# Combine step of a fused attention and mixture layer: the elementwise product moved from GpSimd to VectorE

## The reference

```python
def _L0_attn_ref(content, Wq, Wk, Wv):          # 16 heads of 64
    Q = (content @ Wq).reshape(b, n, HEADS, HEAD_DIM)
    ...
    alpha = jax.nn.softmax(scores, axis=-1)
    alpha = jnp.where(causal, alpha, 0)          # masked after the softmax
    Y = jnp.einsum('bhqk,bkhd->bqhd', alpha, V).reshape(b, n, d)

def _L0_ffn_ref(...):                            # 8 gated experts round one causal attention, D = 128
    ...
    final = jnp.einsum('td,edc,te->tc', attn_out, o_proj, m * routing_weights)

xn = _layernorm(x, axis=-1)
s = _L0_attn_ref(xn, Wq, Wk, Wv)
g = _silu(_L0_ffn_ref(xn, sim_matrix, gates, q_proj, k_proj, v_proj, o_proj))
x = x + s * g
```

## Time and profile before

| | us |
|---|---|
| median of 2 runs | 3610.29 (3608.92 to 3611.66) |
| the profiled execution, its time | 3607.75 |
| its span on the slowest core (core 3), first to last instruction | 3606.2 |
| spans of the 8 cores | 3596.3 to 3606.2 |
| busy in the span: TensorE, VectorE, ScalarE, GpSimd | 2543.5, 2252.2, 2116.6, 324.7 |

### The profile page before, as it was taken

One profiled execution on the slowest core, in us unless ns is written; L12 is line 12 of the kernel. 1 busy time (PEld: TensorE's weight loads), 2 busy tenths in 40 slices (PEclk: granted clock), 3 DMA queues, 4 the chain that ended last, 5 costly groups with the idle time before them and its releaser, 6 DMA issues.

```text
span 3606.2 us, 59910 instructions; the slowest of 8 cores (3596.3 to 3606.2 us)
## 1 busy us (share of the span) xinstructions
PE 2543.5 (71%) x18642; PEld 1154.0 (32%) x18642; DVE 2252.2 (62%) x5858; ACT 2116.6 (59%) x2466; POOL 324.7 (9%) x738
## 2 busy tenths in 40 slices
PE   2179997673887777778778777777878777754430
PEld 1134444331333333333333333333333333321210
DVE  7457773232466766776676677677667667754542
ACT  0000005320277977986897797789679769965541
POOL 0100000000000100010010010001001000122233
PEclk9999998897888778778867867876886787655555
DMA  5510000114000000000000000000000000022334
GB/s 151 141 36 1 1 1 1 65 50 166 12 3 4 6 6 3 4 7 3 4 9 3 3 6 6 4 4 7 2 4 6 6 3 4 7 72 97 119 132 143
DMA packets 35777, 117.12 MB, mean 32 GB/s; under 512 B 5778, under 2 KB 5778, under 8 KB 35474
## 3 DMA queue, kind: packets, MB, share of 16 engines
q1 hardware_dynamic: 22738, 71.34, 5.6%
q0 software_dynamic: 12736, 41.95, 4.2%
HBM read 79.72 MB, written 33.55 MB: 31 GB/s over the span
## 4 chain that ended last, share of the span: by engine, by line
PE 31%; ACT 20%; DVE 17%; issue 15%; DMA 9%; DVEq 4%; POOLq 2%; POOL 1%; ACTq 0%; SPq 0%
ACT expC L1344 6%; ACT stagef L1359 6%; PE PB L889 5%; PE PB L903 5%; PE PB L874 5%; DVE cacc L1083 4%; PE PB L803 4%; DMA KTt<-s_sp 4%; PE PB L806 3%; PE PB L818 3%; PE PB L761 3%; ACT stagef L1344 3%; ACT R L1359 3%; DVE tmpc L1207 3%; POOLq L574 2%
## 5 line engine op out<-in xcount | busy, mean ns | idle before, releaser
L1207 DVE TENSOR_REDUCE tmpc<-stagef 128x2 f32<-128x1024 bf16 (+2 forms) x726 | 811.3, 1126 | 246.3 <-ACT stagef L1359 180.1
L1344 ACT ACTIVATE expC<-PB 128x1024 bf16<-128x1024 f32 x768 | 863.6, 1125 | 87.2 <-PE PB L889 87.2
L1359 ACT ACTIVATE stagef<-PB 128x1024 bf16<-128x1024 f32 x600 | 676.3, 1127 | 240.0 <-PE PB L903 138.4
L889 PE MATMUL PB<-R 64*128 64x512 bf16 x1152 | 296.4, 503 | 274.8 <-ACT stagef L1359 158.9
L1207 DVE TENSOR_REDUCE tmpc<-R 128x2 f32<-128x1024 bf16 (+2 forms) x362 | 406.1, 1122 | 117.6 <-ACT R L1359 89.5
L1344 ACT ACTIVATE stagef<-PB 128x1024 bf16<-128x1024 f32 x384 | 434.8, 1132 | 72.8 <-PE PB L889 72.8
L1359 ACT ACTIVATE R<-PB 128x1024 bf16<-128x1024 f32 x296 | 334.0, 1129 | 104.3 <-PE PB L903 58.4
L889 PE MATMUL PB<-QTt,KTt 64*128 64x512 bf16 x1152 | 283.7, 481 | 147.9 <-ACT stagef L1359 78.6
L683 PE MATMUL PB<-R,xnT 128*128 128x512 bf16 x1536 | 338.3, 380 | 1.0 <-DVE lnat L1000 0.9
L903 PE MATMUL PB<-R 64*128 64x512 bf16 (+3 forms) x1088 | 261.7, 473 | 50.2 <-ACT expC L1344 20.8
L1324 ACT ACTIVATE expC<-PB 128x512 bf16<-128x512 f32 x144 | 74.8, 612 | 364.0 <-PE PB L727 363.9
(11 more groups left out here) (162 smaller groups left out, 3012.0 us busy)
## 6 DMA issues: line engine op xcount, KB each, us to landing
stagef<-x SPq DMA_DIRECT2D x64, 512.0 KB, 4.2
out<-Vau SPq DMA_DIRECT2D x32, 512.0 KB, 4.5
g_sp<-stagef SPq DMA_DIRECT2D x32, 256.0 KB, 2.0
s_sp<-s_stage POOLq DMA_DIRECT2D x64, 128.0 KB, 2.4
QTt<-g_sp POOLq DMA_DIRECT2D x32, 256.0 KB, 3.0
KTt<-s_sp POOLq DMA_DIRECT2D x32, 256.0 KB, 4.1
R<-qp POOLq DMA_DIRECT2D x8, 512.0 KB, 5.2
R<-kp POOLq DMA_DIRECT2D x8, 512.0 KB, 4.8
```

Source lines behind the costliest of these rows:

```text
L889: last = e.matmul(POOL[it["slot"]][:, h * 512:h * 512 + 512], stat, mv, start=True, stop=True, tile_position=(64 * h, 0))
L1207: e.tensor_reduce(s.tmpc[:].rearrange("p (h c) -> p h c", h=2)[:, :, c:c + 1], s.c1scr((m1 - 1) % 3)[:, 0:2 * kw] .rearrange("p (h k) -> p ...
L1344: e.activation(s.expCs(es), PB[[0, 1, 3][it["slot"]]][:, :], AF.Exp).then_inc(sem["aC2"], 1)
L1359: e.activation(scr[:, 0:1024], pbsrc[:, 0:1024], AF.Exp).then_inc(sem["aC1"], 1)
```

## The change

GpSimd no longer waits for the two loads and no longer multiplies: for each tile it issues the two loads and goes on. VectorE waits for the two loads itself, multiplies `KT` by `QT` into `xnb`, drains, and adds as before. The condition under which GpSimd may issue the loads (`vCM` at least k2 - 1) is the same as before, and so are SyncE's list, the buffers and the two slots. The semaphore `gCM` is no longer used.

```diff
 def vector_cmb_one(self, e, j, b):
         e.wait_ge(sem["dCX0" if sl == 0 else "dCX1"], 16 * (k2 // 2 + 1))
-        e.wait_ge(sem["gCM"], k2 + 1)
+        e.wait_ge(sem["dCG0" if sl == 0 else "dCG1"], 16 * (k2 // 2 + 1))
+        e.wait_ge(sem["dCS0" if sl == 0 else "dCS1"], 16 * (k2 // 2 + 1))
         if k2 >= 2:
             e.wait_ge(sem["dOut0" if sl == 0 else "dOut1"], 16 * (k2 // 2))
+        e.tensor_tensor(s.xnb[:, sl * 1024:sl * 1024 + 1024],
+                        s.KT[:, sl * 1024:sl * 1024 + 1024],
+                        s.QT[:, sl * 1024:sl * 1024 + 1024],
+                        ALU.mult)
+        e.drain()
         e.tensor_tensor(vauo[:, sl * 1024:sl * 1024 + 1024],
                         s.xnb[:, sl * 1024:sl * 1024 + 1024],
                         xb[sl], ALU.add).then_inc(sem["vCM"], 1)
...
 def gpsimd_cmb_q(self, e, j):
             e.dma_start(s.KT[:, sl * 1024:sl * 1024 + 1024],
                         sr[:, i, :]).then_inc(sem["dCS0" if sl == 0
                                               else "dCS1"], 16)
-            e.wait_ge(sem["dCG0" if sl == 0 else "dCG1"], 16 * (k2 // 2 + 1))
-            e.wait_ge(sem["dCS0" if sl == 0 else "dCS1"], 16 * (k2 // 2 + 1))
-            e.tensor_tensor(s.xnb[:, sl * 1024:sl * 1024 + 1024],
-                            s.KT[:, sl * 1024:sl * 1024 + 1024],
-                            s.QT[:, sl * 1024:sl * 1024 + 1024],
-                            ALU.mult)
-            e.drain().then_inc(sem["gCM"], 1)
```

## The result

The changed kernel took 3518.17 us (median), the kernel before 3611.03 us beside it. The ratio is 0.9738, with a 95% interval of 0.9726 to 0.9750: 2.6% faster. The medians differ by 92.9 us, where the prediction said 114. The profiled execution has its slowest core at 3516.4 us (core 2) against 3606.2, so 89.8 us less.

The account below looks back on a forecast made before the run. A chain of latencies in the last head pair's combines was taken as the bound: 202.4 + 9.5 us of waits removed, less 73 remaining, less 24.6 of VectorE work, is 114; 3607.75 - 114 = 3494 us, range 3470 to 3530.

Parts of the forecast that it names:

- 202.4 + 9.5 of waits removed: Last head pair: VectorE's 202.4 us of waits for GpSimd's drain and 9.5 us for ScalarE would go.
- A: Combines of the last head pair: two tiles in flight, slightly slowed; 3480 to 3510 us, most likely 3494; chance 0.65.
- Rival B: Combines: DMA becomes bound, 3510 to 3537 us; sign: waits naming `out` or over 4 us at tiles 2, 3; chance 0.16.
- The path: Last head pair: VectorE's 202.4 us of waits set the time; windows between combines, with ScalarE full, keep their length.
- The product: VectorE, each of 32 tiles: product 0.69 us and drain 0.08, 24.6 us of added work in all.
- Block 1: Combine of block 1: VectorE's 9.5 us wait for ScalarE, behind GpSimd's late masks, would go.
- E: Each block's combine: the moment the normalization ends, from which times count; four tiles forecast to end 21.6 us later.
- The waits that remain: VectorE's waits for loads in the eight combines: 7 x 8.6 + 12.9 = 73 us.
- Tile 2 needs x, which is what lands last: Third tile of a block: x takes 5.3 us to land, plus 1.0 for sharing; a wait of 2.4 us.
- Rival C: Combines: transfers faster than in the kernel before, as the product no longer spaces them badly; 3471 to 3480 us; chance 0.10.
- Rival D: Combines: each tile still costs a full round trip, only the shorter product gains, 55 us, giving 3553 us; chance 0.06.
- Rival E: Combines: VectorE's operations hold up GpSimd's load issues, 4.0 us per tile, 128 in all, giving 3622 us; chance 0.03.

Follow-up runs that it names:

- e10_two_early: Changed kernel, two tiles in flight, but GpSimd issues loads once the product of two tiles earlier is through, not its addition; ratio 0.9758, 3508.71 us profiled.
- e3_no_x: Changed kernel with 30 of the 32 loads of x left out; ratio 0.9671, 3484.64 us profiled.
- e2_serial: Changed kernel with one tile in flight: GpSimd issues loads only after the previous tile's addition; ratio 0.9999, 3609.44 us profiled.
- e9_serial_early: Changed kernel with one tile in flight, loads issued once the previous tile's product is through, not its addition; 3551.97 us profiled.
- e1_ahead: Kernel before with the product left on GpSimd, but the next tile's loads issued ahead, two tiles in flight; ratio 0.9842, 3543.82 us profiled.
- e4_sp_queue: Changed kernel with the loads of g and s issued by SyncE instead of GpSimd; ratio 0.9720, 3509.25 us profiled.

## Why the prediction was right, and by how much it was not

The sum reads, with what was measured on the slowest cores: 202.4 + 9.5 of waits removed, less 98.1 that remain, less 24.6 of product and drain: 89.2 us, and the profiled spans differ by 89.8. So every term but one had its size. That one term moved the time out of the band of the forecast: 3518.17 us is outside A's 3480 to 3510, which had 0.65, and inside B's 3510 to 3537, which had 0.16. It lies within the whole range of 3470 to 3530 only because that range took in most of B.

- **The path.** Right. The waits of VectorE in the last head pair were on the path in full, and the stretches between the combines kept their length (148.0 and 146.7 us in all) with ScalarE full.
- **The product.** 690 ns and 0.08 for the drain (3239.88 + 0.69 to 3240.65), as taken. This agrees with the Trainium skill's rate for two bf16 inputs ("VectorE: DVE Perf Modes", the perf-mode tier table) and with its 150 fixed cycles.
- **Block 1.** Right. The first mask stands 15.0 us behind E (13.9 forecast), and the wait of 9.5 us for ScalarE is gone: no sum waits over 1.5 us for ScalarE there.
- **The waits that remain.** Wrong in size: 98.1 us in place of 73. On core 2, 56.8 us fall on the first tiles (47 forecast) and 41.3 on the others (26 forecast). On the other seven cores these are 48.9 to 57.0 and 37.3 to 42.2 us. So the second part was too small on every core, and the first by 2 to 4 us on four cores and by 10 on two, the slowest among them. The second part is the step "Tile 2 needs x, which is what lands last", with 1.0 and 1.5 us added for sharing: from the end of tile 0 to the start of tile 2's product the sum had 6.8 us, and the eight blocks took 7.2 to 9.0, 8.1 in the mean. I had read the landing of s, 3.0 to 4.4 us, off rows in which it was issued ahead of the store and of the load of x; in the changed kernel it is issued behind them, and lands in 5.9, so that most tiles wait for s and not for x. The order of the issues is one part of the miss: restored with two tiles in flight (e10_two_early), it brings this stretch to 7.0 us, but takes only 9 us off the waits behind the first tiles. The larger part is the bytes: a third of them left out (e3_no_x) brings the stretch to 5.8 us and takes off 23. With one tile in flight the order weighs more: e2_serial and e9_serial_early differ only in when the loads are issued, with a landing of 5.4 against 4.3 us and 3609 against 3552 in all.
- **Rival B** (DMA becomes the bound in a combine) has the time, and about half of the mechanism. Of its sign, waits of over 4 us at tiles 2 and 3, half is there: on core 2 tile 2 waits 3.0 to 5.6 us, over 4 in four of eight blocks, and tile 3 at most 2.0. The rest of what speaks for it: the share in the second half of a combine is 0.87, e3_no_x gets 26 us of waits back for fewer bytes, and the four tiles end 24.8 us behind E, nearer to B's 25.4 than to A's 21.6. But the landings did not double to 10.6 us, as B had worked out: that of x is 5.4 us, 5.3 before. The Trainium skill ("DMA: Bandwidth & Descriptors", Specifications) gives about 358 GB/s of HBM per core with both cores of a pair at work. The window of 14 us shows 296 GB/s at a share of 0.87, which is below it; single microseconds show 385 to 414, above it (last section), so this trace does not show 358 as a limit.
- **Rival C** (transfers faster than before) did not occur for any load: s lands in 5.9 us against 4.1 and x in 5.4 against 5.3; only the store is shorter, 3.6 us against 4.5.
- **Rival D** was a real share of the gain: its 55 us is what e9_serial_early got with one tile in flight, where the loads kept their place ahead of the store. In the change itself that place is lost, so the parts do not add: overlap alone 64 us (e1_ahead), product alone 0 (e2_serial) or 56 (e9_serial_early), together 90 by the profiled executions.
- **Rival E** did not occur. GpSimd's L571 took 0.54 us while the product ran (3243.01, the product from 3242.92 to 3243.60), as alone, and with SyncE issuing the loads (e4_sp_queue) the waits are the same. The lock in the Trainium skill ("SBUF — State Buffer", the section on its two separate sides) was not seen for these operations: all 32 issues of L571 took 0.54 to 0.55 us. That section has a two-input VectorE operation take the lock only against a GpSimd operation that reads SBUF.

What stays open is why the first tile of a block, whose two loads share the engines of their own core only with the two of the second tile, waited 7.5 to 8.6 us in blocks 5, 4 and 2 on core 2, and 5.8 to 6.4 in most blocks on cores 0, 3 and 4. Transfers of the other cores would fit, but no run isolates them.

## What to carry to other kernels

When two engines are released by the same event, look at who issues which transfer first: with one tile in flight, a load that lands in 4.3 us ahead of a megabyte of traffic lands in 5.4 behind it, and issuing it there undid the whole worth of a faster product. With two tiles in flight the same reordering was worth little (e10_two_early), because the bytes of both tiles had to pass anyway. A landing time taken from a trace holds only for the place in the order at which it was measured. And when a wait for a load remains, ask first whether the load must be issued that late at all: loading ahead into memory that had become free, with the fresh columns taken from where they had just been written, was worth as much again as the whole change.

## What was not expected of the hardware

- The multiplication of two 128 x 1024 bf16 tiles takes 2109 ns on GpSimd and 690 ns on VectorE, 3.1 times as long.
- DMA moved 385 to 414 GB/s in some single microseconds of a combine and 164 to 270 in others at the same full share (1.02 and more), so that a full share of the engines is not one rate:

```profile
3243.00:3244.00 1.00, 0.00 (x0) 0.00 (x0) 0.93 (x3) 0.85 (x1) 0.55 (x2) 0.50 1.02 385
...
3246.00:3247.00 1.00, 0.03 (x2) 0.00 (x0) 0.03 (x1) 0.82 (x1) 0.56 (x2) 0.50 1.03 201
...
3249.00:3250.00 1.00, 0.05 (x2) 0.00 (x0) 0.00 (x0) 0.00 (x0) 0.00 (x0) 0.50 1.03 414
```

- Issuing two loads 1.2 us earlier in 24 tiles (the first of each block waits for other data) took 57 us off the kernel, which is more than the 24 x 1.2 = 29 us that the moved issue itself explains. The 24 tiles wait 49 us less (130.9 on core 5 of e2_serial, 81.8 on core 2 of e9_serial_early): the 1.1 us by which the median landing of s is shorter makes up 26 of them. Another 6 us lie on the first tiles, 54.8 and 48.7.
